# A linear-recurrence block and its quantised FFN: from chunk 0's fc1 to chunk 2's h, four steps change engine or place

## What is computed

```python
pre = layernorm(x) @ W + b;  i_pre, f_pre, o_pre, z = split(pre)
i = 10 * tanh((i_pre + input_bias) / 10);  f = -softplus(f_pre)
m_next = max(f + m, i)                       # per step, 2048 of them
c = exp(f + m - m_next) * c + exp(i - m_next) * tanh(z)
n = exp(f + m - m_next) * n + exp(i - m_next)
h = sigmoid(o_pre) * c / (n + 1e-6)
x = x + h / sqrt(mean(h * h) + 1e-8) * scale
...
w1, w2 = (q - 128) * scales                  # per group of 128 rows
x = x + 0.5 * (silu((layernorm(x) * gamma + beta) @ w1 + b1) @ w2 + b2)
```

## Time and profile before

| | |
|---|---|
| median of 3 runs | 313.07 us (312.94 to 313.12) |
| profiled execution: time, span | 313.88 us, 311.9 us |
| granted TensorE clock, mean | 0.995 |
| busy TensorE / VectorE / ScalarE / GpSimd | 95% / 85% / 75% / 41% |
| VectorE busy in 81 to 96, 96 to 110, 110 to 135 us | 14.42 of 15, 13.52 of 14, 24.54 of 25 us |

### The profile page before, as it was taken

The page is one execution under the profiler, slowest core; times in us unless marked ns, Lnnn a source line. Parts: engine busy times, 40 slices in busy tenths (PEclk is TensorE's granted clock), DMA queues, the critical chain, the costliest instruction groups (busy, mean ns, idle before and its releaser), DMA issues.

```text
span 311.9 us, 4767 instructions
## 1 busy us (share of the span) xinstructions
PE 295.4 (95%) x1728; PEld 255.2 (82%) x1728; DVE 265.1 (85%) x476; ACT 233.3 (75%) x376; POOL 126.5 (41%) x135
## 2 busy tenths in 40 slices
PE   8799999979899899999998999999999979989996
PEld 6578788856798689987896889988899869879886
DVE  3798989999899999999989998899979998863531
ACT  1599988789879985899694987699875777941930
POOL 0234057320182519611970159111999365154000
PEclk9999999799999999999999999999999999999999
DMA  7980003060000021003000110010000100200101
GB/s 267 344 295 7 0 1 69 0 134 0 2 1 2 12 76 51 0 34 103 1 2 34 39 64 0 0 39 31 1 2 0 67 2 0 69 0 2 68 0 67
DMA packets 11238, 14.73 MB, mean 47 GB/s; under 512 B 848, under 2 KB 10320, under 8 KB 10960
## 3 DMA queue, kind: packets, MB, share of 16 engines
q1 hardware_dynamic: 10368, 12.07, 11.4%
q0 software_dynamic: 288, 1.57, 2.5%
q10 hardware_dynamic: 560, 0.79, 0.7%
HBM read 8.67 MB, written 4.19 MB: 41 GB/s over the span
## 4 chain that ended last, share of the span: by engine, by line
PE 31%; DVE 22%; POOL 19%; issue 12%; ACT 11%; DMA 4%; ACTq 0%; POOLq 0%; DVEq 0%; SPq 0%
POOL rows L1156 4%; POOL g L1141 4%; ACT y L573 4%; PE mm_ps L236 4%; PE mm_ps L238 4%; PE mm_ps L237 4%; DVE y_lo L852 4%; PE z_ps L236 3%; PE z_ps L238 3%; PE z_ps L237 3%; DVE g L820 3%; POOL r L1134 2%; DVE rows L828 2%; DVE bn L833 2%; DMA s<-fc_scale_cols 2%
## 5 line engine op out<-in xcount | busy, mean ns | idle before, releaser
L236 PE MATMUL z_ps<-w_hi,y_hi 128*128 128x256 f32 x248 | 71.3, 288 | 2.4 <-DVE y_lo L852 2.4
L238 PE MATMUL z_ps<-w_hi,y_lo 128*128 128x256 f32 x248 | 70.0, 282 | 0.0
L237 PE MATMUL z_ps<-w_lo,y_hi 128*128 128x256 f32 x248 | 69.9, 282 | 0.0
L573 ACT ACTIVATE y<-mm_ps,b_all,unit 128x512 f32<-128x512 f32 x60 | 46.1, 769 | 11.4 <-PE mm_ps L329 9.7
L236 PEld LDWEIGHTS z_ps<-w_hi,y_hi 128*128 128x128 f32 x248 | 46.8, 189 | 4.0 <-DVE y_lo L852 3.7
L852 DVE TENSOR_TENSOR y_lo<-y,y_hi 128x512 fp32r<-128x512 f32 x64 | 42.8, 684 | 6.9 <-ACT y_hi L576 6.8
L237 PEld LDWEIGHTS z_ps<-w_lo,y_hi 128*128 128x128 f32 x248 | 46.9, 189 | 0.4
L238 PEld LDWEIGHTS z_ps<-w_hi,y_lo 128*128 128x128 f32 x248 | 46.8, 189 | 0.0
L322 PE MATMUL mm_ps<-gt_hi,w_hi 128*128 128x512 f32 x124 | 39.9, 403 | 1.6 <-ACT y L573 1.6
L236 PE MATMUL mm_ps<-xt_hi,wg_hi 128*128 128x512 f32 x96 | 38.4, 400 | 1.1 <-ACT f_gate L505 1.1
L576 ACT ACTIVATE y_hi<-y 128x512 fp32r<-128x512 f32 x60 | 37.9, 632 | 1.9
(11 more groups left out here) (176 smaller groups left out, 653.9 us busy)
## 6 DMA issues: line engine op xcount, KB each, us to landing
out<-rows SPq DMA_DIRECT2D x15, 256.0 KB, 2.1
rows<-x SPq DMA_DIRECT2D x7, 512.0 KB, 7.4
q<-fc_q SPq DMA_DIRECT2D x2, 1024.0 KB, 11.6
wg_raw<-fc_scales SPq DMA_DIRECT2D x1, 1024.0 KB, 6.4
w_lo<-q POOLq DMA_DIRECT2D x1, 1024.0 KB, 7.0
wg_raw<-w_gates SPq DMA_DIRECT2D x1, 512.0 KB, 6.4
wg_raw<-w_gates ACTq DMA_DIRECT2D x1, 512.0 KB, 6.6
w_lo<-q POOLq DMA_DIRECT2D x1, 512.0 KB, 4.7
```

What stands on the lines that cost most here:

```text
L236: pe.matmul(dst, wh[w_at], ah[a_at], start=start, stop=False)
L237: pe.matmul(dst, wh[w_at], al[a_at], start=False, stop=False)
L238: return pe.matmul(dst, wl[w_at], ah[a_at], start=False, stop=stop)
L573: act.activation(y[:, j % YBUFS], fc1_bank(c, j), ACT.Silu, bias=b1_all[:, j:j + 1], scale=unit[:, j:j + 1]).then_inc(silu_done, 1)
```

## The change

1. w2_lo is one subtraction on VectorE (128x2048), between chunk 1's `mean_square` and `h_scaled`; GpSimd's negation and its DMA are gone.
2. Chunk 3 takes its z tiles in the places 2 and 3 and its f tiles in the places 4 and 5. ScalarE takes the two z ahead of the load of the sigmoid table; `maximum(3)` waits for the sixth gate tile.
3. ScalarE's first two silus of chunk 0 stand back to back, and their two copies to y_hi behind them.
4. `h_turned(2)` on TensorE and `square_sums(2)` on ScalarE come one fc1 tile later, behind the sixth; on VectorE `y_low` of tile 3 goes ahead of `mean_square(2)`.

```diff
+Z_SOONER = [0, 1, 4, 5, 2, 3, 6, 7]
+def tile_of(c, j):
+
+    return Z_SOONER[j] if c == 3 else j
...
-                    f = slice(GATE_ORDER[j] * P, GATE_ORDER[j] * P + P)
+                    f = slice(GATE_ORDER[tile_of(c, j)] * P, GATE_ORDER[tile_of(c, j)] * P + P)
...
-                            pe.wait_ge(w2_ready, 16)
+                            pe.wait_ge(w2_ready, 1)
...
-            fc1(1, range(2, 5))
+            fc1(1, range(2, 6))
             h_turned(2)
-            fc1(1, range(5, KF))
+            fc1(1, range(6, KF))
...
-            silu(0, range(0, 4))
+            silu_alone(0, range(0, 2))
+            for j in range(2):
+                act.wait_ge(silu_done, at(0, 8, j + 1))
+                act.activation(y_hi[:, j], y[:, j], ACT.Copy).then_inc(y_hi_done, 1)
+            silu(0, range(2, 4))
             silu_alone(0, range(4, KF))
             square_sums(1)
+            gates(3, range(2, 4))
             act.preload_act_table_set("sigmoid_and_others")
-            gates(3, range(2, GJ))
+            gates(3, range(4, GJ))
...
-            silu(1, range(2, 5))
+            silu(1, range(2, 6))
             square_sums(2)
-            silu(1, range(5, KF))
+            silu(1, range(6, KF))
...
-                dve.wait_ge(gate_done, at(c, 8, 4))
+                dve.wait_ge(gate_done, at(c, 8, 6 if c == 3 else 4))
...
             mean_square(1)
+            dve.wait_ge(w2_rounded, 2)
+            dve.tensor_tensor(w2_lo[:], w2_f, w2_hi[:].bitcast(F32), ALU.subtract).then_inc(w2_ready, 1)
             h_scaled(1)
...
-            y_low(1, range(2, 3))
+            y_low(1, range(2, 4))
             mean_square(2)
-            y_low(1, range(3, 4))
             final(0, 0)
...
-            pool.wait_ge(w2_rounded, 2)
-            negated(w2_lo[:], w2_hi[:], w2_negated)
-            whole_added(w2_lo[:], w2_f, w2_negated, w2_ready)
             rms_root(1)
```

More of the change, by code:

```diff
@@ L171, in layer @@
         w2_scaled, w2_rounded, w2_ready = (sem(n) for n in ("w2_scaled", "w2_rounded", "w2_ready"))
-        w1_negated, w2_negated = sem("w1_negated"), sem("w2_negated")
+        w1_negated = sem("w1_negated")
         beta_w1, b1_ready = sem("beta_w1"), sem("b1_ready")
@@ L500, in gates @@
                     act.wait_ge(pre_done, at(c, 8, j + 1))
[L501 to L507, removed]
+                    m = tile_of(c, j)
+                    bias, tile = gate_bias[:, m:m + 1], gate_bank(c, j)
+                    if m in I_TILES:
+                        ins = act.activation(capped(c)[:, m], tile, ACT.Tanh, bias=bias, scale=1.0 / CAP)
+                    elif m in F_TILES:
+                        ins = act.activation(f_gate[:, s, m - 2], tile, ACT.Sigmoid, bias=bias, scale=-1.0)
+                    elif m in Z_TILES:
+                        ins = act.activation(rec[s][:, 2, m - 4], tile, ACT.Tanh, bias=bias)
                     else:
-                        ins = act.activation(o_gate[:, s, j - 6], tile, ACT.Sigmoid, bias=bias)
+                        ins = act.activation(o_gate[:, s, m - 6], tile, ACT.Sigmoid, bias=bias)
                     ins.then_inc(gate_done, 1)
```

## The result

| | median us | runs | ratio, 95% interval |
|---|---|---|---|
| before | 313.07 (312.59 to 313.14) | 5 | |
| changed | 314.66 (314.34 to 314.79) | 5 | 1.0049 (1.0037 to 1.0062) |

The medians lie 1.6 us apart; by the ratio the changed kernel is slower by 1.5 us, 0.49%. The forecast was 314.5, slower by 1.45.

What follows compares the result with a forecast made beforehand. VectorE's chain was taken to bound the kernel: -1.46 (negation), +2.3 and the held root less the hole (together +0.5), +1.34 (squares), -0.37 (root beside final) gave +1.45, 314.5 us; 8-in-10 range 313.4 to 315.5.

Steps and rivals of the forecast that it cites:

- What bounds: From 100 us to h_turned(4) at 170.82, VectorE and what hangs on it come last; TensorE, 95% busy, has slack.
- Part 1: VectorE's carry copy at 61.89 us no longer waits for GpSimd's negation: all up to mean_square(1) comes 1.46 us sooner.
- Part 2: The w2_lo subtraction on VectorE behind mean_square(1) takes 2.3 us, partly filling a 1.16 us hole.
- Part 3: rms_root(1) on GpSimd ends 0.9 us behind the two-input subtraction, so h_scaled(1) starts 0.5 us later.
- Part 4: TensorE starts fc2(0) 2.3 us sooner, then waits 1.9 us for g at g_turned(1), leaving 0.35 us of lead.
- Part 5: ScalarE's square_sums(2) comes 1.34 us later; rms_root(2) beside final gives 0.37 back; h_scaled(2) is 1.45 us later.
- The sum: VectorE is 1.45 us late at h_scaled(2), with no hole to absorb it up to h_turned(4): 314.5 us.
- The rival in which the root isn't held: rms_root(1) isn't delayed by the subtraction, h_scaled(1) is 0.4 us sooner; sum +0.57, 313.6 us; chance 0.10.
- the rival with TensorE in command: VectorE's lateness is absorbed from 110 to 170 us and TensorE's lead decides: 312.7 us, or 310.8; chance 0.16.
- The rival of one more held power: One more GpSimd root is held by a VectorE product, adding up to 0.9 us: 315.4 us; chance 0.12.

Runs made afterwards that it cites:

- z_and_silus: Kernel before with only chunk 3's z tiles ahead of f and the two silus back to back: 313.38 us, ratio 0.9999.
- te_extra: Kernel before with four extra 128x512 matmuls on TensorE in chunk 5's gates, output unchanged: 313.34 us, ratio 1.0006.
- neg_halves: Kernel before with GpSimd's negation of w2_hi cut into two halves, the DMA the same: 312.57 us, ratio 0.9980.
- sub_halves_h: Changed kernel with the w2_lo subtraction in two halves and h_turned(2), square_sums(2), y_low of tile 3 back in place: 312.30 us, ratio 0.9968.
- h_as_before: Changed kernel with h_turned(2), square_sums(2) and y_low of tile 3 back where they stood before: 313.83 us, ratio 1.0019.
- only_sub: Kernel before with only w2_lo as one VectorE subtraction behind mean_square(1), GpSimd's negation and DMA gone: 313.72 us, ratio 1.0022.
- sub_halves: Changed kernel with the w2_lo subtraction cut into two 128x1024 instructions, one behind the other: 313.45 us, ratio 1.0008.

## Why the prediction was right

- **What bounds.** VectorE's chain, not TensorE. Right: z_and_silus and te_extra show from both sides that TensorE's time isn't passed on, and neg_halves, which edits nothing on TensorE, that time given back to VectorE is.
- **Part 1, the negation: 1.46 us back to VectorE.** mean_square(1) is at +20.95 against +22.22, so 1.27 sooner in the changed kernel; in sub_halves_h, at 77.75 with the common instruction at 56.99, it is at +20.76, the full 1.46. What ate the 0.2 lies with ScalarE, which in the changed kernel waited 0.9 us for TensorE's i gate at a low clock (below). h_as_before, the same program up to there but with a shorter spell at that clock, has mean_square(1) at +20.78.
- **Part 2, the subtraction: 2.3 us.** 2.29.
- **Part 3, the held root: +0.5 us at h_scaled(1).** 0.66, that is 0.5 and the 0.2 of part 1; h_as_before and only_sub, with the short spell, have 0.49 and 0.47. The root ended 0.86 behind the subtraction, forecast 0.9. The rule of the Trainium skill (SBUF — State Buffer, Who interferes with whom) that was cited there held, and sub_halves shows that the hold is for the VectorE instruction under way.
- **Part 4, TensorE's lead and a new wait at g_turned(1).** Right in kind, too large in size: fc2 started at 80.65, +23.65 against +25.48 before, 1.8 us sooner where 2.3 were forecast, and the new wait is 1.4 us where 1.9 were. TensorE's longer spell at half clock took most of the difference: in h_as_before, where the spell is short, fc2 starts at +23.24, 0.10 behind the end of the subtraction and 2.2 us sooner than before, and the wait for g is 1.7. It cost the kernel nothing, since TensorE waits there anyway. The row in the changed kernel:

```profile
80.65 0.28 PE L243 MATMUL z_ps<-w_hi,y_hi 128*128 128x256 f32 x1
```

- **Part 5, the later squares: +1.34, and 0.37 back from the root beside final.** The rows have mean_square(2) at +50.84 against +48.85, 1.99 later (0.66 and 1.33), and the root at 1.04 instead of 1.41. h_scaled(2) is 1.62 later, forecast 1.45; the excess is part 1's 0.2.
- **The sum.** 1.45 forecast, 1.5 measured. The closeness is in part luck: in the rows the loss is 1.62 at h_scaled(2), 1.51 at h_turned(4) and 1.36 at the last instruction, and the runs alone leave 1.2 to 1.9. That nearly nothing of it is absorbed by 170 us was argued from the chain, and the changed kernel's chain shows it. One step of the path was less certain than the prediction has it: it takes the load of x as what chunk 5's layernorm waits for. In the kernel before that load ended at 118.46, and VectorE's scans ahead of the layernorm at 115.95 + 2.45 = 118.40; in the changed kernel the chain reaches the layernorm over the scans, which end at 119.26. The two are as good as tied, and both are as late as VectorE. The rival in which the root isn't held is ruled out by its row of 2.98 us; the rival with TensorE in command by the two experiments. The rival of one more held power isn't seen: from 86 to 125 us GpSimd's instructions take as long as before within 0.02 us, but for the root that got shorter.

## What to carry to other kernels

Before moving work onto an engine, look at which tiny instruction of another engine is issued while it runs: here a 128x4 root that waits for the end of one long two-input instruction turned a 1.16 us hole into a loss, and the same work in two pieces gave the loss back. A TensorE that is 95% busy need not bound anything; follow the chain to the next place where it waits, and see whose lateness ends that wait. A step moved to fill a TensorE stall (h turned one tile later) has to be priced on the engine that reads its result, here 1.34 us of ScalarE work put ahead of the squares.

## Not expected

- The granted clock of TensorE fell to half (1.2 of 2.4 GHz) at the end of the 32 matmuls of one column each (shifted_bias) or right behind them, in every profiled execution, and for unlike times. In two-microsecond stretches from 52 us on it was 1.00, 0.75, 0.50, 0.89, 1.00 in the kernel before and 0.83, 0.50, 0.50, 0.50, 0.96 in the changed one, where what stands ahead of it is the same. fc1's first matmul started at +4.16 instead of +2.57. This difference between a short spell and a long one doesn't reach the end of the kernel: the last instruction is at +254.14 in the kernel before and at +254.26 in z_and_silus, with the short spell, and at +254.21 in te_extra, with the long one.
- A spell as such can reach the end. Of the 76 executions of the kernel before that were run beside the experiments, the nine with a mean granted clock of 1.000 have spans of 310.3 to 310.5 us, the 64 between 0.988 and 0.995 have 310.7 to 312.9 (median 311.3), and the three at 0.984 have 312.2 to 312.6. With the negation in halves and the z tiles and silus moved (neg_halves_z_silus), the two at 1.000 have 310.2 and 310.5, no less than its other four (310.0 to 310.5). So the hold by the whole negation may well be missing where the clock never fell, since w2_hi, and with it the negation, would come sooner (its second half ended at +3.01 with the short spell of the kernel before and at +4.32 with the long one of the changed kernel). No such execution has a trace, and this is not shown.
- Where that spell was long, GpSimd's negation began at 61.70 us, behind the carry's copy, which then took 0.17 us (te_extra). No time was won: the hold fell on VectorE's next scans. Its row there, where 2.45 us is usual:

```profile
62.47 4.11 DVE L778 TENSOR_TENSOR_SCAN rec<-f_gate,carry,rec 128x512 f32<-128x512 f32 x2
```
